# Attention on four batches, one core: far key columns left out, 220 score units for 256, output products in column strips, a step table of its own

## The reference, cut to what matters

```python
x = L0_attn_x                                        # (4, 1024, 128)
x = x + 0.5 * ffn(layernorm(x))                      # first half
x = x + attention(layernorm(x))
x = x + 0.5 * ffn(layernorm(x))                      # second half
out = x

def attention(x):                                    # 16 heads of 8 channels
    q, k, v = split(x @ qkv_w.T); q, k = rotary(q), rotary(k)
    attn = q @ k.T * 8 ** -0.5
    attn += minimum(key - query, 0) * slopes[head] * 8
    return (softmax(attn) @ v) @ proj_w.T + proj_b

def ffn(x):                                          # 8 experts of 64, 2 chosen, and a shared layer of 512
    routed = sum over the two chosen e: score[e] * (relu(x @ fc1_w.T @ w1[e].T) ** 2 @ w2[e].T) @ fc2_w.T
    return routed + relu(x @ up_w.T) ** 2 @ down_w.T
```

## Time and profile before

| what | us |
|---|---|
| median of 3 runs | 788.84 |
| lowest and highest of them | 786.97, 2228.0 |
| span of the profiled execution | 786.6 |
| of it the head, to the first exponential | 78.1 |
| the 256 units, to the start of the tail | 668.2 |
| the tail | 40.2 |

### The profile page before, as it was taken

The page is one execution under the profiler, slowest core; times in us unless marked ns, Lnnn a source line. Parts: engine busy times, 40 slices in busy tenths (PEclk is TensorE's granted clock), DMA queues, the critical chain, the costliest instruction groups (busy, mean ns, idle before and its releaser), DMA issues.

```text
span 786.6 us, 14489 instructions
## 1 busy us (share of the span) xinstructions
PE 740.7 (94%) x5542; PEld 372.4 (47%) x5542; DVE 434.7 (55%) x1162; ACT 611.9 (78%) x497; POOL 204.4 (26%) x174
## 2 busy tenths in 40 slices
PE   5996999999999999999999999999999999999967
PEld 4884443444444444344443443444444454444446
DVE  4677525747756746646357537455464454545344
ACT  3684788878788878878889788688888888888814
POOL 1015221332233322432223322322213113231310
PEclk9998799999999999999999999999999999999989
DMA  7014412022153221033112200223130200200100
GB/s 250 1 37 145 116 47 63 15 87 72 44 141 96 53 81 31 5 106 94 38 41 63 85 5 18 86 61 87 45 100 8 58 2 5 61 5 18 41 14 18
DMA packets 40942, 46.09 MB, mean 59 GB/s; under 512 B 9122, under 2 KB 27146, under 8 KB 40738
## 3 DMA queue, kind: packets, MB, share of 16 engines
q1 hardware_dynamic: 39058, 43.70, 20.3%
q10 hardware_dynamic: 1808, 1.39, 0.6%
HBM read 25.48 MB, written 19.32 MB: 57 GB/s over the span
## 4 chain that ended last, share of the span: by engine, by line
PE 74%; ACT 16%; issue 3%; DVE 2%; DMA 1%; POOL 1%; SPq 0%; POOLq 0%; DVEq 0%
PE f_acc L979 24%; PE f_scores L960 15%; PE f_bank_o L1102 15%; ACT weights L1334 15%; PE f_bank_h L935 10%; PE f_bank_c L1080 2%; PE f_acc L1102 1%; PE f_bank_h L1137 1%; PE f_scores L935 1%; PE f_bank_h L1004 1%; PE f_bank_c L1045 1%; PE f_bank_c L1056 1%; PE f_bank_c L1047 1%; ACT weights L1328 1%; PE f_bank_h L1035 1%
## 5 line engine op out<-in xcount | busy, mean ns | idle before, releaser
L1334 ACT ACTIVATE weights<-f_scores 128x2048 f32<-128x2048 f32 x248 | 465.8, 1878 | 101.5 <-PE f_scores L960 95.9
L979 PE MATMUL f_acc<-weights,v_res 128*9 128x512 f32 x2048 | 268.7, 597 | 0.6 <-DVE weights L1722 0.6
L1102 PEld LDWEIGHTS f_bank_o<-w_out,f_hid 128*128 128x128 f32 x928 | 115.8, 192 | 97.1 <-issue 89.4
L960 PE MATMUL f_scores<-q_op,k_full 25*128 25x512 f32 (+7 forms) x1408 | 132.7, 412 | 17.7 <-ACT weights L1334 8.5
L1102 PE MATMUL f_bank_o<-w_out,f_hid 128*128 128x128 f32 x928 | 137.7, 289 | 0.0
L1722 DVE TENSOR_TENSOR weights<-weights,ediag 128x512 f32<-128x512 f32 x128 | 92.0, 719 | 71.8 <-ACT weights L1334 64.3
L1371 POOL TENSOR_TENSOR f_hid<-f_hid,f_relu 128x512 f32<-128x512 f32 x52 | 76.2, 1466 | 163.2 <-DVE f_hid L1587 163.2
L1371 POOL TENSOR_TENSOR f_hid<-f_relu 128x512 f32<-128x512 f32 x52 | 58.4, 1125 | 203.1 <-ACT f_relu L1248 203.1
L960 PEld LDWEIGHTS f_scores<-q_op,k_full 25*128 25x128 f32 (+1 forms) x1408 | 60.9, 185 | 84.9 <-ACT weights L1334 57.4
L1587 DVE TENSOR_TENSOR f_hid<-f_relu,f_bank_c 128x512 f32<-128x512 f32 x54 | 37.0, 685 | 95.1 <-ACT f_relu L1248 64.8
L935 PE MATMUL f_bank_h<-xn_t,w_hi 128*128 128x512 f32 x224 | 84.5, 459 | 1.4 <-DVE xn_t L1487 1.4
(11 more groups left out here) (241 smaller groups left out, 721.5 us busy)
## 6 DMA issues: line engine op xcount, KB each, us to landing
q_parts<-f_parts SPq DMA_DIRECT2D x24, 256.0 KB, 3.0
k_parts<-f_parts SPq DMA_DIRECT2D x24, 256.0 KB, 3.1
q_op<-q_parts SPq DMA_DIRECT2D x48, 96.0 KB
k_full<-k_parts SPq DMA_DIRECT2D x48, 96.0 KB
o_scratch<-f_o_out SPq DMA_DIRECT2D x124, 18.0 KB
x_ln<-in_L_attn_x_dram SPq DMA_DIRECT2D x8, 256.0 KB, 3.3
rope<-const_rope SPq DMA_DIRECT2D x1, 2048.0 KB, 10.2
x_scratch<-f_res SPq DMA_DIRECT2D x8, 256.0 KB, 2.4
```

The costliest lines, as they stand in the source:

```text
L960: last = nc.tensor.matmul(scores[:, j, lo:hi], k_full[rows, g, kt * P:(kt + 1) * P], q_op[rows, g, CHUNK * half + lo:CHUNK * half + hi], s ...
L979: last = nc.tensor.matmul(acc[BLOCK * j:BLOCK * j + VW, :], v_res[:, c // HALVES, kt, col:col + VW], weights[:, n % WEIGHTS, j, :], start= ...
L1102: last = nc.tensor.matmul(made[:, t * P:(t + 1) * P], hid[:, m, t * P:(t + 1) * P], w_out[:, m, :], start=(m == 0 and t == (2 * side if jo ...
L1334: nc.scalar.activation(weights[:, n % WEIGHTS, :, :], scores[:, :, :], ACT.Exp).then_inc(exps_done, 1)
```

## The change

Heads 0 to 3 (group column g = 0) now look back over 64 positions beyond the key tile, heads 4 to 7 over 256, the others over all (`REACH`). Of a key tile, query columns that lie farther ahead are left out of scores, exponential and weighted sum. A group is now a list of units, each of one or two pieces (key tile, first column in the bank, width): in the first half g = 0 has 7 units and g = 1 has 8, in the second half 3 and 5; the other groups keep 8. That makes 220 units, of which 12 are narrower than 512 columns (448, 384 and 256, four of each) and 16 hold two pieces. The first unit of such a group is the key tile that all 512 queries need. The reference's terms that are left out are those that the bias makes small; `bound_ok` now also asks that each head's bound be within a limit made of its slope and reach (20 for heads 3 and 7).

Each pair of outputs, outside the head and job C of chunk 7, is made as 8 products of 128x32 by 128 columns (`STRIPS`), each into its own 32 partitions, in place of two full ones; and in a step the pairs stand before the hidden products. The table `PLAN` is another one: 36 steps shorter, with jobs spread otherwise.

```diff
+STRIPS = [slice(BLOCK * j, BLOCK * (j + 1)) for j in range(GH)]
+REACH = (64, 256, SEQ, SEQ)
...
+def width_of(half, g, kt):
+
+    return min(max((kt + 1) * P + REACH[g] - CHUNK * half, 0), CHUNK)
+
+
+TOGETHER = {(0, 0): ((3,), (0, 1), (2,), (4,), (5,), (6,), (7,)), (1, 0): ((7,), (3, 6), (4, 5)),
+            (0, 1): ((3,), (0,), (1,), (2,), (4,), (5,), (6,), (7,)), (1, 1): ((7,), (5,), (6,), (3,), (2, 4))}
...
-    ("A", 2, dict(front=(0, 0, 0), norm=(100, 118, 122, 216), route=(217, 218, 219, 220, 221), coef=222, hidden=(217,
-        218, 221, 222, 225, 226, 227, 231), spread=(225, 226, 227, 231), outs=(219, 219, 220, 220, 223, 223, 224, 224, 228,
...
+    ("A", 2, dict(front=(0, 0, 0), norm=(101, 118, 125, 215), route=(215, 216, 217, 218, 219), coef=220, hidden=(213,
+        214, 215, 216, 217, 218, 220, 221), spread=(222, 223, 224, 225), outs=(216, 216, 217, 217, 218, 218, 219, 219,
...
-                for lo, hi, ahead in pieces(limit, CHUNK):
-                    for j in range(GH):
-                        rows = slice(BLOCK * j, BLOCK * j + (FREE_ROWS if ahead else ROWS))
-                        last = nc.tensor.matmul(scores[:, j, lo:hi], k_full[rows, g, kt * P:(kt + 1) * P],
-                                                q_op[rows, g, CHUNK * half + lo:CHUNK * half + hi],
-                                                start=True, stop=True)
+                for piece in unit.pieces:
+                    kt, at = piece.kt, piece.at
+                    limit = min(max((kt + 1) * P - CHUNK * half, 0), CHUNK)
+                    for lo, hi, ahead in pieces(limit, piece.width):
+                        for j in range(GH):
+                            rows = slice(BLOCK * j, BLOCK * j + (FREE_ROWS if ahead else ROWS))
+                            last = nc.tensor.matmul(scores[:, j, at + lo:at + hi], k_full[rows, g, kt * P:(kt + 1) * P],
+                                                    q_op[rows, g, CHUNK * half + lo:CHUNK * half + hi],
+                                                    start=True, stop=True)
...
                 for t in (2 * side, 2 * side + 1):
-                    last = nc.tensor.matmul(made[:, t * P:(t + 1) * P], hid[:, m, t * P:(t + 1) * P], w_out[:, m, :],
-                                            start=(m == 0 and t == (2 * side if job.ends else 0)), stop=(m == HT - 1),
-                                            skip_group_check=True)
+                    for strip in ([slice(0, P)] if job.head or job.ends else STRIPS):
+                        last = nc.tensor.matmul(made[strip, t * P:(t + 1) * P],
+                                                hid[:, m, t * P + strip.start:t * P + strip.stop], w_out[:, m, :],
+                                                start=(m == 0 and t == (2 * side if job.ends else 0)), stop=(m == HT - 1),
+                                                skip_group_check=True)
...
                 for job in JOBS:
+                    for i in range(2 * HT):
+                        if job.outs[i] == step:
+                            outputs(job, i)
+                for job in JOBS:
                     for m in range(HT):
                         if job.hidden[m] == step:
                             hidden(job, m)
-                for job in JOBS:
-                    for i in range(2 * HT):
-                        if job.outs[i] == step:
-                            outputs(job, i)
...
-                nc.scalar.activation(weights[:, n % WEIGHTS, :, :], scores[:, :, :], ACT.Exp).then_inc(exps_done, 1)
+                nc.scalar.activation(weights[:, n % WEIGHTS, :, 0:width], scores[:, :, 0:width],
+                                     ACT.Exp).then_inc(exps_done, 1)
```

More of the change, by code:

```diff
@@ L625, in diagonals_through @@
 def diagonals_through(n):
-    group, c, g, kt = quad_of(n)
-    first = TILES * (c % HALVES)
-    return TILES * group + min(max(kt + 1 - first, 0), TILES)
+    return sum(on_diagonal(unit.c, piece.kt) for unit in UNITS_OF_ALL[0:n + 1] for piece in unit.pieces)
 def fused(nc, sem, env):
```

284 lines of the change are left out of this document (170 added, 114 removed).

## The result

The changed kernel takes 747.24 us (median of 4 runs, 741.3 to 750.14), the kernel before 790.68 in the same comparison. The ratio is 0.9456 with a 95% interval of 0.9401 to 0.9511: faster by 5.4%. The forecast was 741.5 in a range of 724 to 768.

A forecast was written before the change was run, and what follows sets the result against it. ScalarE and TensorE alternate in the units; the bound was to pass to TensorE. 78.1 + 609 + 5 + 2 + 4.5 + 40.2 + 2 - 1.5 gave 739.5, plus 2.2: 741.5, range 724 to 768.

The forecast's parts named there:

- The step rule: A unit step costs the greater of ScalarE's 2.49 us and TensorE's 0.43 + 0.98 + 0.20 plus its products.
- The units, 619: The stretch of 220 units takes 609 + 5 + 2 + 4.5 - 1.5 us.
- Order and waits, 4.5: Units: VectorE runs late at three dense places and stops at one residual; 4.5 us added, bounds 0 and 15.
- Strips, 0.44 a pair: Units: an output pair made in strips of 32 columns stays at 0.44 us, bounds 0.42 and 0.88.
- Full products in this order only 1 to 2 us slower: Units: the new order with full products in place of strips would cost only 1 to 2 us more.
- The case of up to 13 us less by saved drains: Units: some 130 steps could each save 0.1 us of array draining; cheaper case 728 us, chance 0.08.
- The rival that strips' loads can't run under matmuls: Units: strips don't overlap, a pair costs 0.88 us, and the kernel is slower at 821; chance 0.08.
- The head, 0 for both effects: Before the first scores: moved products make it 2 us late, 1.65 us at the fourth exponential may go; both taken as 0.
- The 1.5 taken off the sum: Subtracted from the sum of 741 as the third step's share of the rest, giving 739.5.
- the rest of 5 us: Units: the old table sums to 663 against 668.2 measured; the 5 us left, mostly the third step, were added.
- The tail, 42: After the last unit: the chain of spreads and products on VectorE is 1 to 3 us longer, 2 taken.
- VectorE as the bound: Units: VectorE bounds the dense places, diagonals and weighted sums late; 15 to 25 us more, 755 to 765; chance 0.12.

The follow-up runs named there:

- The two runs with few products: Most output products of the middle jobs left out: in the changed kernel 725.94 us, in the kernel before 779.79 us.
- the busy head: The changed kernel with twelve unread products on TensorE in the head, ahead of the second norms' product: 743.89 us, ratio 0.9425.
- the base: The changed kernel run again with no edit: 746.05 us, ratio 0.9436 to the kernel before.
- the run without diagonals: The changed kernel without VectorE's diagonal products and TensorE's wait for them: 741.97 us, ratio 0.94.
- the moves: The changed kernel with four local edits (residual sum, a spread, a query/key product, operand loads put at other places): 744.02 us, ratio 0.9419.

## Why the prediction was right, and where it was off

The forecast of 741.5 was 0.8% under 747.24, the sign and the range held, and the main point stands: ScalarE saved 36 turns, 95 us by the forecast's sum, and the stretch of units is 44.9 shorter, so TensorE took about half of it back. Step by step:

- *The step rule* (the greater of 2.49 and TensorE's sum): right. Steps with two pairs and a hidden product were forecast at 3.19, and their median is 3.22; two pairs and a q or k product, 3.18. Steps with a hidden product alone, or two pairs alone, stay at 2.49. The two runs with few products agree once their relief is sized at 34 us.
- *The units, 619*: 623.3. Errors of opposite sign, so part of the closeness is luck. Norms' products behind pairs were priced with a change into the full array (0.20 a step) that their steps don't show. Against that stands the clock, which the sum had nowhere: the first three steps took 11.9 us where the busy head made it 8.5, and steps 200 to 211 took 32.5 where it was 29.1. The shift rows (0.3 us of TensorE idle here, 1.55 in the base) were not foreseen either.
- *Order and waits, 4.5*: the places are worth 2.6 (VectorE, by the run without diagonals) and 2.7 (a doubled spread and a doubled q/k product, by the moves): 5.3. The size was near, one reason wrong: the residual sum at step 363 is not what stops unit 146.
- *Strips, 0.44 a pair*: right. Two pairs take 0.98 with the change behind them. "Full products in this order only 1 to 2 us slower" was low: 3.7 by the medians, 2.2 of it from the norms' steps. The case of up to 13 us less by saved drains did not come: in most steps strips only move the change from one side of the products to the other. The rival that strips' loads can't run under matmuls is out: a pair would have been 0.88. The Trainium skill has the rule that changing the tiling mode drains the array (TensorEngine Tiling (Array Packing), Key Properties). The trace agrees, with about 0.1 us for each change.
- *The head, 0 for both effects*: this is the term that failed, by 3.4 us in the profiled run. The products moved there were forecast at 3 x 1.4 + 1 = 5.2 us, and with the whole clock they take 4.98. But TensorE had idled 3.05 us, stood at half clock, and they took 7.67. From the first squares to the first exponential the kernel before takes 16.0 us, the changed kernel 20.3 (base 19.6), with a busy head 17.3 to 17.7. The first three steps take 9.9, 11.9 (base 9.7) and 8.5. So with the whole clock the two effects nearly cancel, 1.3 to 1.7 lost and 1.4 gained, as the forecast had it; without it the loss in the head grows to 4.3 and the gain at the first units goes (base) or turns into a loss (steps of 4.44 and 4.12). I argued that more work before the first scores keeps the array busy, and did not look at the gap ahead of that work, nor at the clock of the rows that I read: the 4.14 us step was itself at half clock.
- *The 1.5 taken off the sum*: the forecast sets both effects of the head at 0 and then subtracts 1.5 for the third step, which is one of them. It also calls the rest of 5 us "mostly the third step", of which its own 1.65 is a third. That is 1.5 of the 5.7 us that the forecast was low.
- *The tail, 42*: 42.4.
- *What would show it*: the units' stretch (610 to 625), the tail and the strips' price came as said. "PE above 95% busy in the units" did not: 582.5 of 623.3 is 93.5%, since about a third of the steps (72 of 219) are still on ScalarE's turn, and TensorE idles in the stalls besides. "ScalarE's wait for scores longer in total" did not by its own line (92.5 for 95.9), because a third of the waiting now stands at the rectifier. The first exponential came at 81.54, past the 81 named as a sign of being wrong, and rightly so for the head; in the base it came at 79.59.
- *VectorE as the bound*: out, 2.6 us by the trace and 4 by the times.

What stays open: why the start of the first squares varies by 3.5 us between executions (58.4 to 61.9) and the wait for the shift rows between none and 1.55; how much of the 41 us the units alone would bring; and whether the stall at unit 146 goes without leaving work out, since the instruction moved there was the wrong one.

## What to carry to other kernels

When two engines alternate, taking work from one gives back only what the other can follow: sum both engines' prices step by step, and price the change between tiles and the full array once per change, not once per instruction. When instructions move to a new place, look at what their engine did just before that place: here TensorE ran at half speed for 10 to 17 us behind such a gap, and a few useless products in the gap delayed nothing. Before crediting an edit with a wait that is gone, look whether the wait is there in every execution without the edit. A wait that seems to have shrunk may have moved to the instruction in front of it, so add up all waits of an engine.

## What the runs showed of the hardware

- Filling idle time with unread products raised the mean granted clock of the whole execution from 0.965 to 0.978 (four runs of the base) to 0.987 to 0.992 (four runs) and was worth 8 us of 746. That is more than the strips and their order (3 to 5).
- The fall of the clock differs between executions of one program. After the gap in the head it came back at 90 us in one profiled run and at 83 in another, and in the latter it fell once more at 509 us, behind 0.99 us of idleness, for one step of 3.56 us instead of 2.49. That is a part of the spread of 741 to 750; the start of the first squares and the shift rows are others.
- A product whose loaded part is 16 columns wide goes behind column strips without the cost of a change: it starts 0.34 us earlier than behind whole products.
- Two records of 128 columns in one strip take 0.22 us; sixteen in four strips take 0.44. A strip alone is half the price of four.
- VectorE's diagonal product took 1.49 us while a GpSimd product of two SBUF tensors ran beside it, and 0.68 three microseconds later without one. Over the whole trace, the 84 that meet no square on GpSimd take 0.70 us in the mean, and the three that overlap one for 1.22 us take 1.76 to 1.77.
